# Layer 0 of a two-layer graph attention kernel: the engines' loop covers rounds 4 to 63 instead of 6 to 61

## The reference

```python
h = relu(layernorm(x))                      # layer 0
e = (h @ Ws) @ (h @ Wt).T
x = x + softmax(where(adj > 0, e, -9e15)) @ (h @ Wc)
h = relu(layernorm(x))                      # layer 1
Wh = h @ W
e = leaky_relu((Wh @ a1)[:, None] + (Wh @ a2)[None, :], 0.2)
x = x + elu(softmax(where(adj > 0, e, -9e15)) @ Wh)
```

## Time and profile before

| | us |
|---|---|
| three runs | 1413.15, 1419.63, 1412.64 |
| median | 1413.15 |
| the profiled execution, device time | 1424.22 |
| its span, first to last instruction | 1422.4 |
| PE busy | 1279.6 (90%) |
| DVE busy | 1251.1 (88%) |
| ACT busy | 1026.3 (72%) |
| mean granted TensorE clock | 0.971 |

### The profile page before, as it was taken

How to read it: one execution, slowest core, us unless ns; L and a number is a source line. 1 busy time by engine, 2 the same in 40 slices (tenths; PEclk the granted TensorE clock), 3 DMA queues, 4 the chain that set the end, 5 groups by cost and what they waited for, 6 DMA issues and landing times.

```text
span 1422.4 us, 76006 instructions
## 1 busy us (share of the span) xinstructions
PE 1279.6 (90%) x31819; PEld 1132.5 (80%) x31947; DVE 1251.1 (88%) x2317; ACT 1026.3 (72%) x2035; POOL 32.3 (2%) x75
## 2 busy tenths in 40 slices
PE   5867899999998989999999899889799999999896
PEld 3656788887877878888888788777699989999895
DVE  8877799999888989999999989747799999999896
ACT  5755567666666667676767666558699989999795
POOL 2200000000000000000000000012000000000000
PEclk9979899999999999999999999999899999999998
DMA  6678799999999999999999999531134244334332
GB/s 246 244 267 283 273 363 381 373 367 384 348 346 344 373 380 345 367 385 365 366 375 378 366 357 373 200 127 42 54 107 116 83 122 122 108 91 122 110 89 71
DMA packets 104072, 363.20 MB, mean 255 GB/s; under 512 B 11504, under 2 KB 36336, under 8 KB 70128
## 3 DMA queue, kind: packets, MB, share of 16 engines
q1 hardware_dynamic: 103920, 361.02, 70.3%
HBM read 319.03 MB, written 41.94 MB: 254 GB/s over the span
## 4 chain that ended last, share of the span: by engine, by line
PE 49%; DMA 17%; DVE 14%; issue 12%; ACT 5%; SPq 1%; DVEq 1%; ACTq 0%; POOL 0%; POOLq 0%
DMA arena<-in_adjB 17%; PE ps L869 16%; PE ps L856 10%; PE ps L761 5%; DVE arena L1470 4%; DVE arena L1445 3%; PE ps L729 3%; PE ps L756 3%; PE ps L782 3%; DVE mx L1479 2%; PE ps L717 2%; ACT arena L1118 2%; PE ps L755 1%; PE ps L656 1%; PE ps L658 1%
## 5 line engine op out<-in xcount | busy, mean ns | idle before, releaser
L782 PE MATMUL ps<-arena 128*128 128x129 f32 x2048 | 249.1, 280 | 4.7 <-issue 4.7
L1104 ACT ACTIVATE arena<-ps 128x512 f32<-128x512 f32 x256 | 153.0, 598 | 132.1 <-PE ps L729 131.9
L869 PE MATMUL ps<-arena 128*128 128x129 f32 x2048 | 245.2, 278 | 1.2 <-issue 1.2
L782 PEld LDWEIGHTS ps<-arena 128*128 128x128 f32 x2048 | 240.6, 195 | 5.0 <-issue 5.0
L1445 DVE TENSOR_SCALAR arena<-arena 128x2048 fp8e4<-128x2048 int32 x192 | 235.0, 1224 | 3.9 <-PE ps L744 2.3
L869 PEld LDWEIGHTS ps<-arena 128*128 128x128 f32 x2048 | 236.9, 194 | 1.4 <-issue 1.4
L1688 DVE TENSOR_SCALAR arena<-arena 128x128 f32<-128x128 f32 x768 | 202.9, 346 | 25.0 <-issue 15.2
L1098 ACT ACTIVATE arena<-ps 128x512 f16<-128x512 f32 x256 | 153.9, 601 | 59.7 <-PE ps L717 59.5
L761 PEld LDWEIGHTS ps<-arena 128*128 128x128 f16 x2048 | 139.0, 99 | 64.1 <-issue 5.8
L1479 DVE TENSOR_REDUCE mx<-ps 128x1 f32<-128x1024 f32 x128 | 155.8, 1217 | 33.2 <-PE ps L761 32.6
L729 PE MATMUL ps<-arena 128*32 128x128 f16 x8192 | 166.3, 223 | 16.6 <-issue 10.9
(11 more groups left out here) (165 smaller groups left out, 1446.4 us busy)
## 6 DMA issues: line engine op xcount, KB each, us to landing
arena<-in_adjB SPq DMA_DIRECT2D x256, 1024.0 KB, 7.4
sel_pick<-arena SPq DMA_DIRECT2D x64, 256.0 KB, 9.6
sel<-arena SPq DMA_DIRECT2D x64, 256.0 KB, 9.5
arena<-sel_pick SPq DMA_DIRECT2D x64, 256.0 KB, 3.7
arena<-sel SPq DMA_DIRECT2D x64, 256.0 KB, 2.8
arena<-in_xB SPq DMA_DIRECT2D x4, 1024.0 KB, 6.3
x_t<-in_x SPq DMA_DIRECT2D x64, 64.0 KB, 8.0
x_mid<-y_t SPq DMA_DIRECT2D x64, 64.0 KB, 8.2
```

What stands on the lines that cost most here:

```text
L782: last = nc.tensor.matmul(pv_ps, p_T[:, s * P:(s + 1) * P], v_sel[:, b, s, :], start=False, stop=(s == SB - 1), skip_group_check=True)
L869: last = nc.tensor.matmul(xv_ps[b], w_msk[:, b, s, :], x1_sel[:, b, s, 0:VW], start=False, stop=(s == SB - 1), skip_group_check=True)
L1104: nc.scalar.activation(v_sel[:, b, 4 * g:4 * g + 4, 0:D], vg_ps.rearrange("p (s v) -> p s v", v=D), ACT.Copy).then_inc(v_evac, 1)
```

## The change

`tile_sweep` writes out rounds 0 to 3, loops over rounds 4 to 63 in pairs (30 passes in place of 28), and writes out rounds 64 to 67. SP, which must not load a tile 64, is called with `fetched=False`: it loops over rounds 4 to 61 and writes out 62 to 67.

For the loop to start at round 4, the counts it waits for must be positive there. DVE raises three kinds of semaphores at the start of `constants()` by the counts of two tiles: `y_ready` by 2, `pv_done` by 8, each `y_out` by 16. All waits for them have the same amount added. The dropped waits of the first two tiles are therefore there now, for counts that are already reached. Two steps that were tied to round 4 move into round 3: PE's wait for `rows_ready` (to the end of round 3) and SP's load of `W1` (with its wait for `mean_ready`).

```diff
+        Y0, W0, O0 = 2, 8, 16
-        def tile_sweep(eng, step):
-
-            for i in range(6):
+        def tile_sweep(eng, step, fetched=True):
+
+            full = TILES if fetched else TILES - 2
+            for i in range(4):
                 step(i, i % 2)
-            with eng.Fori(6, TILES - 3, 2) as i:
+            with eng.Fori(4, full - 1, 2) as i:
                 step(i, 0)
                 step(i + 1, 1)
-            for i in range(TILES - 2, TILES + 4):
+            for i in range(full, TILES + 4):
                 step(i, i % 2)
...
-                sp.wait_ge(y_ready, t + 1)
+                sp.wait_ge(y_ready, t + (Y0 + 1))
...
-                if isinstance(i, int) and i == 4:
+                if isinstance(i, int) and i == 3:
                     sp.wait_ge(mean_ready, 1)
                     sp.dma_start(w_sb[:, 0, :], W1).then_inc(w_in, 16)
...
-            tile_sweep(sp, tile_io)
-            sp.wait_ge(y_out[0], 16 * (TILES // 2))
+            tile_sweep(sp, tile_io, fetched=False)
+            sp.wait_ge(y_out[0], O0 + 16 * (TILES // 2))
...
-                wait(pe, y_ready, t - 1)
+                wait(pe, y_ready, t + (Y0 - 1))
...
-                    wait(pe, y_ready, t)
+                    wait(pe, y_ready, t + Y0)
...
-                if isinstance(i, int) and i == 4:
-                    pe.wait_ge(rows_ready, 1)
...
                 if there(i, 2):
                     scores(a, b, 2)
+                if isinstance(i, int) and i == 3:
+                    pe.wait_ge(rows_ready, 1)
...
-                wait(act, pv_done, t * 4 + (g - 7))
+                wait(act, pv_done, t * 4 + (W0 + g - 7))
...
-                wait(act, pv_done, t * 4 + (2 * h - 2))
+                wait(act, pv_done, t * 4 + (W0 + 2 * h - 2))
...
             def constants():
 
+                dve.sem_inc(y_ready, Y0)
+                dve.sem_inc(pv_done, W0)
+                for b in range(2):
+                    dve.sem_inc(y_out[b], O0)
...
-                dve.wait_ge(pv_done, t * 4 + 4)
+                dve.wait_ge(pv_done, t * 4 + (W0 + 4))
...
-                wait(dve, y_out[b], (t - b) * 8)
+                wait(dve, y_out[b], (t - b) * 8 + O0)
...
-                dve.wait_ge(y_ready, t + 1)
+                dve.wait_ge(y_ready, t + (Y0 + 1))
```

More of the change, by code:

```diff
@@ L467, in tile_io @@
                     sp.wait_ge(conv_act, TILES)
-                    sp.wait_ge(y_out[0], 16 * (3 * TILES // 8))
-                    sp.wait_ge(y_out[1], 16 * (3 * TILES // 8))
+                    sp.wait_ge(y_out[0], O0 + 16 * (3 * TILES // 8))
+                    sp.wait_ge(y_out[1], O0 + 16 * (3 * TILES // 8))
                     load_rows(x_midB, 1, range(3))
-                if isinstance(i, int) and i == 4:
+                if isinstance(i, int) and i == 3:
                     sp.wait_ge(mean_ready, 1)
@@ L481, in _ @@
             load_x(1, 1)
-            tile_sweep(sp, tile_io)
-            sp.wait_ge(y_out[0], 16 * (TILES // 2))
-            sp.wait_ge(y_out[1], 16 * (TILES // 2))
+            tile_sweep(sp, tile_io, fetched=False)
+            sp.wait_ge(y_out[0], O0 + 16 * (TILES // 2))
+            sp.wait_ge(y_out[1], O0 + 16 * (TILES // 2))
             load_rows(x_midB, 1, (3,))
@@ L681, in prepare @@
                     if mode == 1 and b == 1:
-                        pe.wait_ge(y_ready, TILES)
+                        pe.wait_ge(y_ready, TILES + Y0)
                     project(b, b, base, mode)
```

## The result

| | before | after |
|---|---|---|
| median of 22 runs | 1415.06 us | 1408.14 us |
| lowest to highest | 1409.88 to 1420.94 | 1401.97 to 1415.59 |
| the profiled execution's span | 1422.4 | 1402.1 |

The ratio after to before is 0.995, 95% interval 0.9934 to 0.9965: 7.1 us faster, between 5.0 and 9.3. In a second set of runs (7 of the changed kernel, 30 of before) it is 0.9955 (0.9938 to 0.9972), 6.4 us. The forecast was 8.6 us less.

What follows compares the result with a forecast made beforehand. The adj stream and its ring were taken to bound the loop, PE's stops for first-time code rounds 4 to 7 and 62. -9.5 - 3.7 + 4.6 = -8.6 us, from 1413.15 to 1404.6 us; range 1399 to 1411, 8 times in 10.

Steps and rivals of the forecast that it cites:

- Rounds 6 and 7 become a second pass: Layer 0's rounds 6 and 7 run loop code already fetched: 35.9 us before, 26.4 after, -9.5 us.
- Rounds 62 and 63 become a loop pass: The formerly written-out rounds 62 and 63 join the loop: 30.1 us before, 26.4 after, -3.7 us.
- The exit's stop moves into round 64, +4.6, wherever it falls, and round 65 keeps its own: Code after the loop still needs fetching: PE stops in round 64, +4.6 us; round 65's 2.08 us stop carried unchanged.
- Rounds 4 and 5 unchanged: Rounds 4 and 5, fetched for the first time before and after, stay at 33.3 us.
- Layer 1 at nothing, bounds -4.7 and +4.7: Layer 1's code lies otherwise in the fetch blocks: no cost; bounds one stop gone or one more.
- The small parts at nothing: DVE's semaphore increments, returned waits, the moved rows_ready wait and W1 load, and SP's shorter loop cost nothing.
- the stops move rather than go: Rival, chance 0.18: rounds 4 and 5 or round 65 get one stop more, +4.6 back: -4.0, 1409 us.
- the slow rival: Rival, chance 0.09: layer 1's blocks fall badly, 4.7 us per added stop; with three, +5.5, 1419 us.
- the refetched loop: Rival, chance 0.02: the loop body is fetched again in each of 29 passes, +75 - 8.6, about 1480 us.
- the adj stream would hold rounds 6 and 7: Rival, chance 0.05: rounds 6 and 7 wait for adj instead, no measurable change, about -4, 1409 us.

Runs made afterwards that it cites:

- Head only: The changed kernel with all engines looping over rounds 4 to 61 and rounds 62 to 67 written out; 0.9973 of before, -3.8 us.
- exit_stream: The changed kernel with the last tile's four adj chunks loaded a second time in round 63, read by nobody; 0.9957 of before.

## Why the prediction was right

The time fell into the range and the change into the interval: 8.6 us forecast, 7.1 measured (5.0 to 9.3). The median, 1408.14 us, is not below the 1406.1 to which the prediction gave 0.62; the interval shows a change clear of nothing all the same, since it is three times as narrow as the 0.5% that the prediction took for the least difference that can be told. The step times below are means of the two traces of each kernel.

- *Rounds 6 and 7 become a second pass*, forecast -9.5: 35.8 to 25.6, **-10.2**. Right, in cause too: waits for issue 6.5 us to none, q8 silent, full pace at once. Head only shows it alone, -9.7. The 26.4 forecast for the two rounds was the pace of the one loop trace that is slow, 13.21 us a round; the others give 12.9 to 13.1.
- *Rounds 62 and 63 become a loop pass*, forecast -3.7: 30.6 to 25.8, **-4.8**. Right; the second trace of before has two long stops there, 2.21 and 2.74 us, so the first was the cheaper.
- *The exit's stop moves into round 64, +4.6, wherever it falls, and round 65 keeps its own*: this step failed. Round 64 has no long stop, that of round 65 grew from 2.08 us to 3.37 (2.8 in the second trace), and the stage costs **+2.8** (35.9 to 38.7). The error was to take the price of a first fetch from rounds 62 and 5, which have the adj stream beside them, for a round without it, the DMA engines at 0.02 in its first 4 us. exit_stream gives round 64 that stream and with it +4.8 (43.5 less 38.7), where the prediction had set down 4.6. The cost that is there, +2.8, is round 65's: its stop, under the load of `x_mid`, is 1.3 and 0.7 us longer, and behind it the float32 weighing starts at the lower clock, 0.51 from 908.9 to 912.0 us, where before had 1.00.
- *Rounds 4 and 5 unchanged*: 32.2 to 33.3, **+1.1**, with 2.3 us between two traces of one kernel. Not told from nothing.
- *Layer 1 at nothing, bounds -4.7 and +4.7*: 391.4 to 393.6, **+2.2**, and it repeats (394.2, 393.1 against 391.2, 391.6). The place of its blocks is worth up to 4.9 us over the kernels above. It could not be had from the rows of before; the bounds held it.
- *The small parts at nothing*: round 3 starts at 84.1 and 83.6 before and at 83.1 and 83.7 after. Right.

The steps add up to -10.2 - 4.8 + 2.8 + 1.1 + 2.2 = -8.9 in the traces, forecast -8.6: the exit and layer 1 err by -1.8 and +2.2, and nearly cancel, which is luck. Of the rivals, "the stops move rather than go" is what happened in part, at round 65 and not where it was looked for; layer 1 went the slow rival's way, but by less than one stop; the refetched loop is real, but begins at a body between 1400 and 2800 instructions. That the adj stream would hold rounds 6 and 7 is out. What stays open: why the timed runs give 7.1 and 6.4 where the traces give 8.9 without the loop; the interval holds both, and stops in executions that aren't profiled can't be seen.

## What to carry to other kernels

Look for waits for "issue" in the middle of a row of equal instructions, and hold them against the packets of the instruction queue: code run for the first time costs TensorE up to some 4 us a stop where it is short matmuls beside a full DMA stream, and a loop's first pass counts as such. The stream need not be the main one: round 65's stop comes under 3 MB loaded ahead for the next stage. What it would bring to issue them elsewhere was not tried. Put as many rounds as possible into a hardware loop, keep its body well under what TensorE holds (1400 instructions stayed, 2800 cost 5.6 us a round, 18.6 less 13.0), and price what is left of written-out code by rounds with the same DMA load beside them. Any edit moves all code behind it against the blocks; a few us of difference can be that alone, and 64 to 192 idle waits at the start of a program test it.

## What the runs showed of the hardware

- The granted clock follows the stops: 0.81 and 0.90 in rounds 4 and 5 after, 1.00 in rounds 6 and 7, where PE stood still in the first two and not in the others. It need not be a stop for code: in the loop of before a wait of 3.0 us for the exponentials is followed by 0.50 from 446.9 to 450.2 us. And not every stop is followed by it: behind the 2.08 us in round 65 before it reads 1.00.
- A code fetch suffers from data traffic: at a DMA share of 0.2 the issue waits of two rounds are 0.6 us, at 0.8 they are 6.3, for the same code. The fetch's packet takes 1.1 and 1.2 us; it is its start that comes late, up to 6.2 us after the block's first instruction against up to 2.2.
- A body of two rounds, 1399 instructions, was held over the 29 passes after its first without a packet; one of four rounds fetched 12.75 packets a pass and stood 6.0 us at each branch back.
